# A decoder layer on one core: the passage from cross attention to the feed-forward part, written in another order on TensorE, VectorE, ScalarE and GpSimd

## The reference, cut to what matters

```python
x = x + gated_slot_attention(layernorm(x))                    # 4 heads, a scan over 128 tokens
x = x + cross_attention(layernorm(x), ctx, bias, mask)        # 16 heads of 8 channels
x = x + routed_ffn(layernorm(x))                              # 8 experts that share wi and wo

# cross attention, for one sequence and head
scores = q @ k.T * 8**-0.5 + attn_mask + spatial_bias + directional_bias
probs  = softmax(where(pad, -inf, scores))
out    = (probs @ v) @ Wo.T + bo

# feed-forward part, for one token
top_v, top_i = top_k(softmax(h @ gate_w.T + gate_b), 2)
for e in range(8):
    gate  = (top_i == e).sum() * top_v.sum()
    inter = h @ wi.T + bi + (h @ lora_A[e].T) @ lora_B[e].T   # 512 wide, rank 16
    out  += gate * (relu(inter) @ wo.T + bo)
```

## Time and profile before

| | |
|---|---|
| profiled execution, device time | 586.37 us |
| its span in the trace | 584.6 us |
| median of the three runs | 587.0 us |
| busy share of the span: TensorE, VectorE, ScalarE, GpSimd | 91%, 82%, 68%, 61% |
| mean granted TensorE clock | 0.987 of full |
| one step of cross attention before the passage | about 7.0 us |
| the passage, from the first norm of a group (425.5) to the router logits of tick 1 (455.0) | 29.5 us |
| one tick of the feed-forward part behind it | about 16.1 us |

### The profile page before, as it was taken

The page is one execution under the profiler, slowest core; times in us unless marked ns, Lnnn a source line. Parts: engine busy times, 40 slices in busy tenths (PEclk is TensorE's granted clock), DMA queues, the critical chain, the costliest instruction groups (busy, mean ns, idle before and its releaser), DMA issues.

```text
span 584.6 us, 16628 instructions
## 1 busy us (share of the span) xinstructions
PE 530.4 (91%) x5328; PEld 408.3 (70%) x5328; DVE 480.0 (82%) x1945; ACT 398.6 (68%) x1033; POOL 355.9 (61%) x362
## 2 busy tenths in 40 slices
PE   4689999999997779999999999999976999999986
PEld 3457777777776547777777777777755877788865
DVE  2578888788778588999999999999988888888862
ACT  2668878878876369999999999999954333333311
POOL 6334555555544899888888888888823443333330
PEclk9899999999999899999999999999989999999999
DMA  5920000000000358889999999999400000000000
GB/s 152 248 43 2 1 1 1 0 0 0 1 1 2 71 108 136 155 155 159 161 164 166 162 159 166 161 163 158 84 2 2 0 20 19 20 18 18 19 18 19
DMA packets 84459, 42.86 MB, mean 73 GB/s; under 512 B 4378, under 2 KB 84132, under 8 KB 84388
## 3 DMA queue, kind: packets, MB, share of 16 engines
q1 hardware_dynamic: 83234, 41.63, 39.0%
q10 hardware_dynamic: 1154, 0.33, 0.2%
HBM read 39.86 MB, written 2.10 MB: 72 GB/s over the span
## 4 chain that ended last, share of the span: by engine, by line
PE 58%; issue 15%; DVE 13%; POOL 5%; ACT 5%; DVEq 0%; POOLq 0%; ACTq 0%
PE banks L925 9%; PE banks L938 9%; PE banks L891 5%; PE banks L458 5%; PE banks L1245 4%; PE banks L904 3%; PE banks L1269 3%; DVE shared L723 3%; PE banks L914 2%; PE banks L449 2%; PE banks L422 2%; PE banks L910 2%; DVE banks L696 2%; DVE shared L702 2%; PE banks L504 2%
## 5 line engine op out<-in xcount | busy, mean ns | idle before, releaser
L1138 POOL TENSOR_TENSOR c_bias<-c_fside,c_cm 128x2048 f32<-128x2048 f32 x32 | 146.4, 4574 | 20.1 <-PE banks L891 18.4
L972 ACT ACTIVATE c_P<-c_P,c_min 128x128 f32<-128x128 f32 x512 | 156.6, 391 | 2.4 <-DVE c_min L1044 2.4
L1044 DVE CUSTOM_DVE_ANT_0 c_P<-banks,c_bias 128x128 f32<-128x128 f32 x512 | 116.3, 284 | 6.5 <-PE banks L891 5.2
L925 PEld LDWEIGHTS banks<-ident,c_P 128*128 128x128 f32 x512 | 57.9, 142 | 32.8 <-ACT c_P L972 21.7
L925 PE MATMUL banks<-ident,c_P 128*128 128x128 f32 x512 | 74.7, 278 | 6.6 <-DVE shared L1080 5.8
L1080 DVE COPY shared<-banks 128x512 f32<-128x512 f32 x96 | 65.7, 684 | 0.0
L1245 PE MATMUL banks<-um,lb_s 128*128 128x512 f32 x192 | 55.6, 405 | 2.7 <-ACT shared L1302 1.9
L1481 POOL TENSOR_TENSOR xs<-shared,xs 128x512 fp32r<-128x512 f32 x8 | 10.8, 1351 | 66.4 <-ACT xs L1312 66.4
L1302 ACT ACTIVATE shared<-banks,bi_col 128x512 f32<-128x512 f32 x32 | 22.0, 688 | 37.9 <-PE banks L1245 37.9
L1245 PEld LDWEIGHTS banks<-um,lb_s 128*128 128x128 f32 x192 | 34.2, 188 | 18.8 <-ACT shared L1302 12.5
L1044 DVE DVE_READ_ACCUMULATOR2_ANT c_min<- 128x1 f32 x512 | 42.6, 83 | 0.0
(11 more groups left out here) (195 smaller groups left out, 1295.3 us busy)
## 6 DMA issues: line engine op xcount, KB each, us to landing
c_fside<-in_fside_Bx16xSxS_dram SPq DMA_DIRECT2D x64, 512.0 KB, 7.4
c_ctx<-in_ctx_dram SPq DMA_DIRECT2D x32, 64.0 KB, 5.5
out_dram<-shared SPq DMA_DIRECT2D x8, 256.0 KB, 2.3
X<-in_x_dram SPq DMA_DIRECT2D x3, 512.0 KB, 5.6
kmask_sb<-in_mask_BxS_bf_dram SPq DMA_DIRECT2D x1, 512.0 KB, 7.0
X<-in_x_dram SPq DMA_DIRECT2D x2, 128.0 KB, 3.3
c_P<-in_L_ffn_wi_dram SPq DMA_DIRECT2D x1, 256.0 KB
c_P<-in_L_ffn_lora_B_dram SPq DMA_DIRECT2D x1, 256.0 KB
```

Of the source, the lines that this page charges most:

```text
L925: last = nc.tensor.transpose(bank(2 + i % 2)[:, 128 * j:128 * j + 128], P[:, q, XG * i + j, :], ident[:])
L972: last = nc.scalar.activation(P[:, par, h, :], P[:, par, h, :], ACT.Exp, bias=mn[:, par, h:h + 1], scale=-1.0)
L1044: last = nc.vector.tensor_tensor_reduce(out=P[:, o, h, :], in0=bank(score_banks(n + 1)[i])[:, 128 * j:128 * j + 128], in1=fm[:, o, h, :], ...
L1138: nc.gpsimd.tensor_tensor(fm[:, q, :, :], fs[:, q, :, :], bc(cm[:], XH), ALU.add).then_inc(C["fm"], 1)
```

## The change

No operation is added or taken away: each engine executes as many instructions as before. The pieces of ticks -1, 0 and 1 and of steps 30 to 32 stand in another order. For that, the tick functions of the feed-forward part take names of pieces in place of the numbers 0 to 3, as the cross attention already did, and `x_low` and the output bias get names of their own on GpSimd. Two waits are new or changed: GpSimd waits until the choices of group 0 are made (`M["hot"]`) before it takes `u_low`, and TensorE's wait for the masked scores (`C["tt"]`) asks for two groups fewer ahead of `x_turned` and for all of them ahead of `choices_turned`. `u_low` and `roots` now stand ahead of `x_low`. The wait for the last addition to the stream (`C["x2"]`) moves on TensorE from the head of tick 1 to its `down`.

```diff
-            if norm and 0 in parts:
+            on = named(only)
+            if on(norm, "statistics"):
                 statistics()
...
-        def f_peeled(tick, t, parts=(0, 1, 2, 3)):
-            tick(t // 2, t % 2, *(0 <= t + k < GROUPS for k in (1, 0, -1)), parts)
+        def f_peeled(tick, t, *names):
+            tick(t // 2, t % 2, *(0 <= t + k < GROUPS for k in (1, 0, -1)), names or None)
... GpSimd
             f_peeled(experts, -1)
             x_peeled(cross, B - 2)
-            f_peeled(experts, 0, (0,))
-            f_peeled(experts, 0, (1,))
-            f_peeled(experts, 0, (2, 3))
-            x_peeled(cross, B)
+            pool.wait_ge(M["hot"], 1)
+            f_peeled(experts, 0, "inner")
+            f_peeled(experts, 0, "roots")
+            f_peeled(experts, 0, "inputs")
+            f_peeled(experts, 0, "bias")
             f_peeled(experts, 1)
... ScalarE
             f_peeled(experts, -1)
-            x_peeled(cross, B - 2)
-            f_peeled(experts, 0, (0,))
+            x_peeled(cross, B - 2, "exps1", "exps2", "exps3", "exps0", "sums")
             x_peeled(cross, B - 1, "exps1")
-            f_peeled(experts, 0, (1,))
-            x_peeled(cross, B - 1, "exps2", "exps3", "sums", "turned3")
-            f_peeled(experts, 0, (2, 3))
+            x_peeled(cross, B - 2, "turned3")
+            f_peeled(experts, 0, "inputs")
+            x_peeled(cross, B - 1, "exps2")
+            f_peeled(experts, 0, "logits")
+            x_peeled(cross, B - 1, "exps3", "sums", "turned3")
             x_peeled(cross, B)
-            f_peeled(experts, 1)
+            f_peeled(experts, 1, "first")
+            f_peeled(experts, 1, "inputs", "logits", "experts")
... VectorE
-            f_peeled(experts, -1)
-            x_peeled(cross, B - 2)
-            f_peeled(experts, 0, (0,))
+            f_peeled(experts, -1, "statistics")
+            x_peeled(cross, B - 2, "scores0", "turned0", "scores1", "turned1")
+            f_peeled(experts, -1, "normalise")
+            x_peeled(cross, B - 2, "scores2", "scores3", "outputs", "turned2", "values")
+            f_peeled(experts, 0, "logits")
+            x_peeled(cross, B - 2, "stream")
             x_peeled(cross, B - 1, "turned0")
-            f_peeled(experts, 0, (1,))
+            f_peeled(experts, 0, "ranks", "choices")
             x_peeled(cross, B - 1, "turned1", "outputs", "turned2", "stream")
-            f_peeled(experts, 0, (3,))
-            f_peeled(experts, 0, (2,))
-            x_peeled(cross, B)
+            f_peeled(experts, 0, "statistics")
+            f_peeled(experts, 0, "inner", "normalise")
+            x_peeled(cross, B, "outputs")
+            f_peeled(experts, 0, "gates")
+            f_peeled(experts, 1, "statistics")
+            x_peeled(cross, B, "stream")
             dve.wait_ge(C["x2"], B)
-            f_peeled(experts, 1)
+            f_peeled(experts, 1, "logits", "experts", "ranks", "choices", "gates", "inner", "normalise")
... TensorE
-            f_peeled(experts, -1)
-            x_peeled(cross, B - 2)
+            x_peeled(cross, B - 2, "scores", "turned0", "turned1", "mix", "turned2", "turned3", "values")
+            pe.wait_ge(C["tt"], 4 * B - 2)
+            f_peeled(experts, 0, "inputs")
+            x_peeled(cross, B - 1, "turned0")
+            x_peeled(cross, B - 2, "outputs")
+            f_peeled(experts, 0, "logits")
+            x_peeled(cross, B - 1, "turned1", "mix", "turned2")
             pe.wait_ge(C["tt"], 4 * B)
-            f_peeled(experts, 0, (0,))
-            x_peeled(cross, B - 1, "turned0")
-            f_peeled(experts, 0, (1,))
-            x_peeled(cross, B - 1, "turned1", "mix", "turned2", "turned3", "outputs")
-            f_peeled(experts, 0, (2,))
-            x_peeled(cross, B)
+            f_peeled(experts, 0, "choices")
+            x_peeled(cross, B - 1, "outputs")
+            x_peeled(cross, B - 1, "turned3")
+            x_peeled(cross, B, "mix")
+            f_peeled(experts, 1, "first")
+            f_peeled(experts, 1, "inputs")
+            x_peeled(cross, B, "outputs")
+            f_peeled(experts, 1, "logits", "experts", "choices")
             pe.wait_ge(C["x2"], B)
-            f_peeled(experts, 1)
+            f_peeled(experts, 1, "down")
```

66 lines of the change are left out of this document (35 added, 31 removed).

## The result

The changed kernel took 584.51 us as the median of 8 runs (581.36 to 585.11), the kernel before 588.29 us in the 8 runs beside it (586.71 to 590.45). The ratio is 0.9918 with a 95% interval of 0.9899 to 0.9936: the change saves 0.82%, about 4.8 us. A second set of runs gave 0.9891 (0.9861 to 0.9922). The forecast of 583.6 was 0.9 us too low and inside its range, and the change stayed within 1% by the first set. But the agreement is in part luck, since it hides errors that cancel. The forecast took 3.4 us off a median of 587.0 from three runs, and eight runs of the kernel before gave 588.29, 1.3 us more; from there the gain was 3.8 us by the medians and 4.8 by the ratio. One term was mis-sized by 0.95 us in favour of the change. And a rival, the fall of TensorE's clock, came true in both profiled executions of the changed kernel and cost 1.6 to 1.7 us in each.

What follows compares the result with a forecast made beforehand. VectorE's list and waits were taken to bound the passage from 425 to 452. Reordering moved tick 1's logits from 454.99 to 451.54, 3.45 us, so the 587.0 us median became 583.6, range 582.4 to 586.4.

Steps and rivals of the forecast that it cites:

- What bounds the passage: From 425 to 452, VectorE's list and its waits hold the kernel; the ticks behind keep 16.1 us each.
- Its ceiling: VectorE's listed waits in the passage, together 4.84 us, are about the most a better order alone could give.
- Step 1, norm: VectorE, group 0: scores and copies fill the 1.49 us root wait; `turned2` starts at 432.63, 1.55 us earlier.
- Step 2, logits: Router logits of tick 0 on VectorE start at 435.45 instead of 438.12, after 2.0 us with nothing to do.
- Step 3, choices: VectorE's ranks and choices in tick 0: L1403 shortened by 0.46 us, choices ending at 441.4.
- Steps 4 to 7: Step 31 outputs to tick 1: `x_low` ends at 447.5, `first(0)` starts at 447.6, logits at 451.54; VectorE's other work fits.
- The sum: VectorE's logits of tick 1 start at 451.54 instead of 454.99, 3.45 us earlier; bounds 2.4 to 3.9.
- The clock rival: TensorE's clock falls in the new passage, slowing `turned0`, outputs and logits: gain 2.0 us, time 585.0; chance 20%.
- The median: Whole kernel: 587.0 us falls to 583.6, chance 55%; eight times in ten between 582.4 and 586.4.
- `x_low` did run beside the inner products: Rival, GpSimd's chain: `x_low` runs behind VectorE's inner products and `normalise`, 2.0 us later; gain 1.4, time 585.6; chance 12%.
- VectorE's wait of step 2 did not eat the gain: Rival: VectorE's 2.0 us logits wait and `outputs` queued behind choices leave gain 0 to 0.8, time 586.6; chance 8%.
- the slow case: TensorE's clock falls before the choices and stays low through the mix and `first(0)`: 5.2 us lost, time 588.8; chance 5%.

Runs made afterwards that it cites:

- The kernel with all of it: Changed kernel plus GpSimd waiting for the gates, router logits ahead of `turned0`, and tick 0's `x_low` ahead of the roots: median 580.21 us, ratio 0.9863.
- the filled kernel: Changed kernel plus eight unread products filling TensorE's pause ahead of `turned0` of step 31: median 582.55 us, ratio 0.9906.

## Why the prediction was right, and where it was not

- **What bounds the passage:** right. All of the difference lies between 425 and the logits of tick 1; the ticks behind it passed the gain on unchanged (129.56 against 129.61 us). Its ceiling, the 4.84 us of VectorE's waits, was wrong. It leaves out a wait of 0.72 us ahead of an output, and it counts idle time only, while 1.4 us of hold-up stood inside VectorE's busy time. The kernel with all of it has a passage 6.15 us shorter (23.34 against 29.49), with the same operations, of which the 3.4 us of low clock in the old one explain at most 1.7. The wait in the profile of the kernel before:

```profile
435.58 0.29 DVE L1084 TENSOR_TENSOR X<-banks,X 128x128 f32<-128x128 f32 x1 [0.72 <-PE banks L915]
```

- **Step 1, norm:** right to 0.05 us (7.18 instead of 7.13 from the first row to the copy `turned2`). With the norm in front that distance is 8.67 or 8.68 us in all profiles, whatever the clock, so the 1.49 us are won whole.
- **Step 2, logits:** right at full clock. From the first row to the logits the forecast had 9.95 us and the filled kernel took 9.91, with 1.85 us of waiting for the 2.0 forecast. In the profiled execution the clock fell there, and it took 11.45.
- **Step 3, choices:** the mis-sized term. The forecast took 0.46 us off, L1403 alone, and left L1404 at 1.64 us without asking after it. It is equally long in all eight ticks of the kernel before (1.64 to 1.67), and it was a hold-up in all eight: alone the operation takes 0.69. The two together went from 2.48 to 1.07 us, so the term is 1.41. In the section of the Trainium skill that the prediction named for L1403 ("SBUF — State Buffer", "SBUF: two separate sides") the rule also names VectorE operations with two inputs in SBUF, and L1404 is one. By the rule it would have to wait for `u_low`, and the rows agree. In tick 0 of the kernel before L1404 ends at 444.14, 0.54 us behind the end of `u_low` at 443.60, and in tick 1 of the changed kernel it ends 0.55 us behind `x_low`. The two rows of the kernel before, VectorE and GpSimd:

```profile
442.50 1.64 DVE L1404 SCALAR_TENSOR_TENSOR shared<-shared 128x512 f32<-128x512 f32 x1
```

```profile
442.15 1.45 POOL L1485 TENSOR_TENSOR shared<-shared 128x512 fp32r<-128x512 f32 x1
```

- **Steps 4 to 7:** right. The wait for the outputs is 0.27 to 0.30, `first(0)` waits for `x_low` and for no other, and 8.11 us instead of 8.18 from the statistics of group 1 to the logits of tick 1.
- **The sum:** 26.04 us for the passage by the forecast, 25.00 to 25.04 with the clock up until the router's logits were through: the 0.95 of L1406 and 0.05 to 0.1 of small parts. With the fall, 26.57 and 26.69. The gain of 4.45 us between 29.49 and 25.04 lies above the range of 2.4 to 3.9 that the prediction gave it; the 3.9 is not worked out there. It also holds a fall of 3.4 us that the old passage had, and no profile shows the kernel before without one. The times at equal clock give 3.1 to 4.0.
- **The clock rival** (20%, 1.4 us on the path): its mechanism came true in both profiles of the changed kernel, at the place it named and for 1.7 us, and the low clock lasted 6.8 us, not 3.4. What it did not weigh is that the kernel before has such falls too, and more of them: its second profile lost 2 us more in the passage than the first, on which the whole sum was built. This goes with the medians being farther apart than the profiles.
- **The median:** 584.51 lies in the range, and that is luck in part. The base was 1.3 us too low, the term for the choices 0.95 us too small, and the low clock, in both kernels, was left out of the sum.
- **The other rivals:** `x_low` did run beside the inner products at 1.27 us; VectorE's wait of step 2 did not eat the gain, though it was worth 1 us to remove; the slow case did not occur in 14 runs.

## What to carry to other kernels

Compare an operation's length with that of another of the same shape on the same engine before taking it as its own: one that is equally long in every round may be equally held up in every round. When two engines exclude each other, taking the meeting away at one place moves it to the next operation of the same kind, so choose what the other engine shall meet, not only what it shall miss. The idle time of an engine is then no ceiling for what a better order can win. And build a sum for a gain of half a percent on more than one profile, and compare runs at equal mean clock.
